# Routing of a mixture-of-experts decoder rebuilt: logits per batch in the norm, expert biases in the tile loop, slot tables in a stage of their own

## The reference, cut to what matters

```
logits = h @ W_router (+ b_router)        # 256 x 8
L0_ffn: one shared expert, 256 -> 1024 -> 256, times the sum of the top-2 weights
L1_ffn: softmax, top 2, renormalised; expert e: (silu(h@W1a+b) * (h@W1b+b)) @ W2[e] + b2[e]
L2_ffn: softmax over all, top 2 kept;     expert e: gelu(h@W1[e]+b1[e]) @ W2[e] + b2[e]
x = x + sum over the two chosen e of weight[e] * expert_e(h)
```

## Time and profile before

| | us |
|---|---|
| median of 3 runs | 3351.38 |
| lowest, highest | 3343.55, 3355.01 |
| profiled execution | 3345.55 |
| its span, first to last instruction | 3343.8 |
| PE busy in it | 2799.0 (84%) |
| DVE busy | 1519.8 (45%) |
| ACT busy | 1294.2 (39%) |
| mean granted clock of PE | 0.900 |

### The profile page before, as it was taken

How to read it: one execution, slowest core, us unless ns; L and a number is a source line. 1 busy time by engine, 2 the same in 40 slices (tenths; PEclk the granted TensorE clock), 3 DMA queues, 4 the chain that set the end, 5 groups by cost and what they waited for, 6 DMA issues and landing times. The chain is left out here.

```text
span 3343.8 us, 57353 instructions
## 1 busy us (share of the span) xinstructions
PE 2799.0 (84%) x18661; PEld 1999.5 (60%) x18662; DVE 1519.8 (45%) x3568; ACT 1294.2 (39%) x3845; POOL 888.0 (27%) x570
## 2 busy tenths in 40 slices
PE   5653899969785989999689977899968998889799
PEld 2352566646454555555379844566637997776466
DVE  5676788840534133333532266665652001653211
ACT  1321677731442113333222221677733332772211
POOL 2351555510001022222113324454521221430000
PEclk8876999979898999999769977999976999898899
DMA  2000100000241010000236620100033555003000
GB/s 100 1 1 1 35 14 14 7 16 12 52 111 31 4 37 15 10 14 7 79 121 236 222 66 7 45 19 18 14 129 104 177 184 165 8 13 107 27 25 22
DMA packets 107205, 189.63 MB, mean 57 GB/s; under 512 B 56020, under 2 KB 81316, under 8 KB 95316
## 3 DMA queue, kind: packets, MB, share of 16 engines
q1 hardware_dynamic: 92834, 162.10, 15.3%
q0 software_dynamic: 6816, 18.62, 1.9%
q10 hardware_dynamic: 7442, 7.47, 0.8%
HBM read 169.46 MB, written 18.71 MB: 56 GB/s over the span
## 5 line engine op out<-in xcount | busy, mean ns | idle before, releaser
L1319 POOL TENSOR_TENSOR L_xattn_p<-L_xattn_p,L_xattn_ri 112x1500 f32<-112x1500 f32 (+1 forms) x192 | 435.8, 2270 | 640.3 <-DVE L_xattn_ri L1577 640.3
L1475 ACT ACTIVATE L_xattn_pT<-ps 125x448 f32<-125x448 f32 (+1 forms) x576 | 254.4, 476 | 371.0 <-PE ps L1393 370.7
L1487 ACT ACTIVATE L_xattn_p<-L_xattn_sa,L_xattn_ng 112x375 f32<-112x375 f32 x512 | 305.0, 598 | 70.4 <-DVE L_xattn_ng L1606 51.7
L1393 PEld LDWEIGHTS ps<-ident,L_xattn_p 112*125 112x125 f32 x1920 | 253.1, 190 | 115.4 <-ACT L_xattn_pT L1475 35.4
L1393 PE MATMUL ps<-ident,L_xattn_p 112*125 112x112 f32 x1920 | 294.7, 284 | 21.2 <-ACT L_xattn_pT L1475 11.3
L979 PEld LDWEIGHTS ps<-L_ffn_xsT,L_ffn_w 128*128 128x128 f32 x2240 | 265.5, 195 | 7.5 <-ACT L_ffn_xsT L1009 2.3
L979 PE MATMUL ps<-L_ffn_xsT,L_ffn_w 128*128 128x128 f32 x2240 | 266.5, 278 | 2.8 <-ACT L_ffn_xsT L1009 2.8
L267 POOL TENSOR_TENSOR ln_rstd<-ln_tmp,half 112x8 f32<-112x8 f32 x26 | 44.3, 1720 | 785.4 <-DVE ln_tmp L220 596.3
L1041 DVE COPY L_ffn_y<-ps 128x256 f32<-128x256 f32 x70 | 29.7, 424 | 374.9 <-PE ps L988 374.9
L988 PE MATMUL ps<-L_ffn_weights,L_ffn_hT 128*128 x840 | 192.9, 380 | 2.1 <-DVE L_ffn_hT L1052 2.1
L278 PE MATMUL ps<-ident,ln_xn 112*128 112x112 f32 x416 | 97.9, 395 | 108.8 <-DVE ln_xn L247 94.3
(11 more groups left out here) (403 smaller groups left out, 5266.5 us busy)
## 6 DMA issues: line engine op xcount, KB each, us to landing
L_ffn_w<-in_L_ffn_experts SPq DMA_DIRECT2D x74, 1024.0 KB, 5.1
L_attn_toeplitz<-L_attn_h SPq DMA_DIRECT2D x4, 3136.0 KB, 22.7
L_xattn_src<-in_ctx SPq DMA_DIRECT2D x32, 281.2 KB, 2.9
L_ffn_weights<-in_L_ffn_experts SPq DMA_DIRECT2D x8, 1028.0 KB, 15.0
L_xattn_src<-in_ctx SPq DMA_DIRECT2D x16, 375.0 KB, 3.0
L_xattn_keys<-in_ctx SPq DMA_DIRECT2D x16, 281.2 KB, 6.7
L_xattn_rows<-in_ctx_rows SPq DMA_DIRECT2D x16, 281.2 KB
L_ffn_weights<-in_L_ffn_experts SPq DMA_DIRECT2D x8, 516.0 KB, 8.5
```

The source lines that it names most:

```text
L1319: g.tensor_tensor(P[:, m % 4, :, :], P[:, m % 4, :, :], ri[:, m % 4, :].unsqueeze(2).broadcast_to([T, W, S2]), ALU.mult).then_inc(s["prob_ ...
L1393: last = pe.transpose(turned(t)[:, j * T:(j + 1) * T], P[:, m % 4, j, kc * KW:(kc + 1) * KW], k.ident[0:T, 0:T])
L1475: act.activation(PT[:, m % 4, kc, :, :].rearrange("p h t -> p (h t)"), turned(t), ACT.Copy).then_inc(s["pt_ev_a"].sem, 1)
L1487: last = act.activation(P[:, n % 4, j, :], at, ACT.Exp, bias=ng[:, n % 4, j:j + 1], scale=-1.0 if mask else 1.0, accum_out=rs[:, n % 4, j: ...
```

## The change

- The norm: with `keep` and no learned scale DVE writes each batch once, straight into `keep`, and PE turns it from there. PE's part is written out instead of looped in these norms and in L0_ffn's. With `per_batch`, PE makes the logits of a batch two batches later, with the batch's turned tokens stationary (112 columns) and the 8 router columns moving, into PSUM bank 6; before the first it waits for the pack.
- `router` keeps only the comparison and the gates; DVE takes the logits from bank 6, adding the bias, which the pack now holds on all partitions.
- `add_second_biases` serves L0_ffn alone. In the routed layers b2 of all experts lies in the pack on all 128 partitions (2048 columns instead of 256), and DVE adds it to each tile's result in `expert_tiles`.
- `list_rows` is the table block alone. In it SP issues the first two first-weight loads and POOL, once the rows stand, the first two row fetches.
- The slots' weights are computed at the start of `expert_tiles`, and ACT makes one unit matrix a tile there, 35 in all.

```diff
@@ layer_norm @@
+        direct = keep is not None and not two_pows
+        xn = None if direct else sb("ln_xn", [T, 4, D])
...
+                        if direct:
+                            v.tensor_scalar(keep[:, b * D:(b + 1) * D], xin, mv[:, 2 * b:2 * b + 1],
+                                            scale[:, b:b + 1], ALU.subtract, ALU.mult).then_inc(ndone.sem, 1)
+                            continue
                         v.wait_ge(*ntr.at(b - 3))
...
+                if direct or per_batch is not None:
+                    lag = 2
+                    for b in range(B + lag):
+                        if b < B:
+                            turn(b, b % 4)
+                        if per_batch is not None and b >= lag:
+                            if b == lag:
+                                pe.wait_ge(*k["pack_in"].at(32))
+                            pe.wait_ge(*nev.at(b - lag + 1))
+                            per_batch(pe, b - lag)
...
+def logits_of(k, E, w):
+
+    def logits(pe, b):
+        for c in range(2):
+            last = pe.matmul(k.ps[0:T, 6, b * E:(b + 1) * E], k.XT[:, c, b * T:(b + 1) * T], w[:, c, :], start=(c == 0),
+                             stop=(c == 1))
+        return last
...
@@ router, on vector @@
-                with v.Fori(0, G // 2) as i:
-                    for u in range(2):
-                        v.wait_ge(*tr.at(2 * i + u + 1))
-                        v.tensor_copy(lg[:, bass.ds((2 * i + u) * GB, GB), :],
-                                      chunks(k.ps[0:T, 2 + u, 0:GB * E], GB)).then_inc(lgd.sem, 1)
-                v.wait_ge(*lgd.at(G))
+                of = chunks(k.ps[0:T, 6, 0:B * E], B)
+                if bias is None:
+                    v.tensor_copy(lg[:, :, :], of)
+                else:
+                    v.tensor_tensor(lg[:, :, :], of, bias.unsqueeze(1).broadcast_to([T, B, E]), ALU.add)
...
+def list_rows(k, route, consts, ahead):
...
+            @block.sync
+            def _(sp):
+                ahead["weights"](sp)
+
+            @block.gpsimd
+            def _(g):
+                g.wait_ge(*s["rg_rows"].at(1))
+                ahead["rows"](g)
+
+            @block.tensor
+            def _(pe):
+                for c in range(4):
+                    pe.wait_ge(*s["rg_hot"].at(c + 1))
+                    for n in range(c * part, (c + 1) * part):
+                        last = pe.matmul(k.ps[0:KT, 6, 0:2 * (most - 1)], place[:, n, :],
+                                         owned[:, n, :, :].rearrange("p w q -> p (w q)"), start=(n == 0),
+                                         stop=(n == picks - 1))
+                last.then_inc(s["rg_listed"].sem, 1)
...
@@ place_tokens @@
-                for n in range(PICKS):
-                    ch.link(v.tensor_tensor(hit[:, :, :], slot[:, :, :],
-                                            pick[:, n:n + 1, :].broadcast_to([T, E, B]), ALU.is_equal))
-                    ch.link(v.tensor_tensor(hit[:, :, :], hit[:, :, :], g3, ALU.mult))
-                    ch.link(v.tensor_reduce(route.weight[:, n, :], by_token(hit), AX.X, ALU.add))
                 ch.link(v.tensor_tensor(two[:, :], pick[:, 1, :], pick[:, 0, :], ALU.is_gt))
-                v.tensor_tensor(route.weight[:, 1, :], route.weight[:, 1, :], two[:, :], ALU.mult)
...
+    def first_weights(sp):
+        for t in range(2):
+            load_first(sp)(t, t)
+
+    def first_rows(g):
+        g.wait_ge(*s["rg_put"].at(16))
+        for t in range(2):
+            fetch(g)(t)
...
@@ expert_tiles @@
-                for n in range(PICKS):
-                    for b in range(B):
-                        act.activation(shares[:, n, b, :], k.ident[0:T, 0:T], ACT.Copy,
-                                       scale=route.weight[:, n, b:b + 1])
+                    act.activation(shares[:, bass.ds(t, 1), :].rearrange("p n t -> p (n t)"), k.ident[0:T, 0:T],
+                                   ACT.Copy, scale=route.weight[:, bass.ds(t, 1)])
+
                 copy_tokens(0, 0)
+                act.wait_ge(*s["rg_weighed"].at(1))
                 in_turn(act, step)
...
                 def copy_y(t, u):
+                    e = expert(mybir.EngineType.DVE, t)
                     v.wait_ge(*s["rg_down"].at(t + 1))
...
-                    v.tensor_copy(y[:, u, :], k.ps[:, 6 + u, 0:D]).then_inc(s["rg_y"].sem, 1)
+                    v.tensor_tensor(y[:, u, :], k.ps[:, 6 + u, 0:D], b2[:, bass.ds(e * D, D)], ALU.add).then_inc(
+                        s["rg_y"].sem, 1)
...
@@ host_ffn, L1_ffn @@
-        small = dict(router=by_rows(w["Wr"]), router_b=w["br"][:, None], b2=w["b2"])
+        small = dict(router=by_rows(w["Wr"]), router_b=on_rows(w["br"]), b2=on_rows(w["b2"]))
```

More of the change, by code:

```diff
@@ L443, in feed_forward, with router @@
                   down_added=n * GB, exp_in0=16 * ((experts + 1) // 2), exp_in1=16 * (experts // 2))
-def router(k, E, w, bias, gates, mode):
+def logits_of(k, E, w):
+    def logits(pe, b):
+        for c in range(2):
+            last = pe.matmul(k.ps[0:T, 6, b * E:(b + 1) * E], k.XT[:, c, b * T:(b + 1) * T], w[:, c, :], start=(c == 0),
+                             stop=(c == 1))
+        return last
+    return logits
+def router(k, E, bias, gates, mode):
     nc = k.nc
@@ L556, in add_second_biases @@
         gT = k.tile(ctx, "gates_turned", [n_g, B, T], F32)
-        if route is not None:
-            picks, part = PICKS * B, PICKS * B // 4
-            most = route.tiles + 2
-            sb = lambda n, sh: k.tile(ctx, n, sh, F32)
-            past, rest, place = sb("past", [T, picks, most]), sb("rest", [T, picks]), sb("place", [T, picks, KT])
-            owned = sb("owned", [T, picks, 2, most - 1])
-            chosen = route.pick[:, :, :].rearrange("p n b -> p (n b)")
-            spare = k.tile(ctx, "spare", [KT, most - 1], F32)
-            marks, ranks, ids, spares = consts
-            along = lambda ap, n: ap.unsqueeze(2).broadcast_to([T, ap.shape[1], n])
         with k.nc.Block(no_gpsimd_drain=True) as block:
@@ L569, in _ @@
             def _(pe):
-                def biases(i):
+                pe.wait_ge(*s["gs_copied"].at(1))
+                for q in range(B // 4):
+                    for j in range(4):
+                        last = pe.transpose(k.ps[0:n_g, q, j * T:(j + 1) * T], gs[:, 4 * q + j, :],
+                                            k.ident[0:T, 0:T])
+                    last.then_inc(s["gt_tr"].sem, 1)
+                for i in range(B // 2):
                     b = 2 * i
@@ L672, in sub_ffn @@
     gates = k.tile(ctx, name + "_gates", [T, spec["experts"] * B], F32)
-    layer_norm(k, pack=(tile, dram, lay["_total"]))
+    E = lay["router"][2] // 2 if "router" in lay else None
+    layer_norm(k, pack=(tile, dram, lay["_total"]), per_batch=E and logits_of(k, E, chunks(p("router"), 2)))
     if spec["mode"] == "fixed":
@@ L761, in __init__ @@
         self.rows = k.tile(ctx, "rows", [KT, 2, self.tiles + 1], mybir.dt.int32)
-        self.weight = k.tile(ctx, "weight", [T, PICKS, B], F32)
+        self.weight = k.tile(ctx, "weight", [T, self.tiles], F32)
+        self.slot = k.tile(ctx, "slot_f", [T, E, B], F32)
         self.expert = k.tile(ctx, "expert", [1, self.tiles + 2], mybir.dt.int32)
@@ L874, in place_tokens, with tile_loads, expert, load_first @@
         k.advance(rg_const=2, rg_chosen=1, rg_counted=1)
-def expert_tiles(k, route, name, weights, dram, layout, hidden, gated, act_fn, shares):
+def tile_loads(k, route, xs, w1, dram, layout):
+    nc, s = k.nc, k.signals
+    first_cols = layout["w1"][2]
+    w_in, x_in = [s["rg_w0"], s["rg_w1"]], [s["rg_in0"], s["rg_in1"]]
+    def expert(eng, t):
+        return nc.values_load(route.expert[0:1, bass.ds(t, 1)], engines=[eng], min_val=0,
+                              max_val=layout["_experts"] - 1,
+                              skip_runtime_bounds_check_because="place_tokens clamps it to the experts")
+    def load_first(sp):
+        def load(t, u):
+            e = expert(mybir.EngineType.SP, t)
+            sp.wait_ge(*s["rg_up"].at(2 * t - 2))
+            sp.dma_start(w1[:, u, :, :].rearrange("p c n -> p (c n)"),
+                         dram[bass.ds(e, 1), :, 0:first_cols].rearrange("e p n -> (e p) n")).then_inc(
+                             w_in[u].sem, 16)
+        return load
+    def fetch(g):
+        def one(t):
+            g.wait_ge(*s["rg_turned"].at(t - 1))
+            g.indirect_dma_start(xs[:, t % 2, :], None, k.rows_x[:, :],
+                                 bass.IndirectOffsetOnAxis(ap=route.rows[:, 0, t:t + 1], axis=0)).then_inc(
+                                     x_in[t % 2].sem, 16)
+        return one
+    def first_weights(sp):
[5 more added lines that the diff above has]
+            fetch(g)(t)
+    return dict(expert=expert, load_first=load_first, fetch=fetch, weights=first_weights, rows=first_rows)
+def expert_tiles(k, route, name, weights, layout, hidden, gated, act_fn, shares, xs, w1, ahead, b2, gates):
```

(5 more changed lines are left out.)

219 lines of the change are left out of this document (85 added, 134 removed).

## The result

The changed kernel takes 3301.83 us (median of 4 runs, 3298.93 to 3302.60), the kernel before 3347.47 on the same chip (4 runs, 3341.96 to 3355.01): a ratio of 0.9861, 95% interval 0.9837 to 0.9884, faster by 45.6 us. Its profiled execution took 3302.05 against 3345.55 before, 43.5 less.

A forecast was written before the change was run, and what follows sets the result against it. PE was taken to bound the routed tile loop (172.87 of 175 us busy), leaving the openings to gain. L0 +3.6, L1 -19.2, L2 -17.6 and L2_attn -7.1 make -40.3; put on the median, 3311 us, range 3290 to 3331.

The forecast's parts named there:

- Part 1: L0, L1, L2 norms: logits at the half clock, 1.12 us a batch; comparison +3.6, -0.3, +1.1 us.
- Part 2: L2_attn's norm, without logits: DVE writes once, 6.3 us against 10.8, -4.5; the following products -2.6.
- The clock's -2.6: Products behind L2_attn's norm: seven passes of 0.75 us instead of 0.37 at the half clock go, -2.6 us.
- Part 3: Placing in L1 and L2: slot-weight instructions leave the chain for the tile block, hidden there; -2.2 us each.
- Part 4: Table block of L1 and L2: without bias products PE's 64 passes stand in one run; -10.8 us each.
- Part 5: Rows to first product: weights and row fetches issued ahead; -5.9 us in L1, -5.7 in L2.
- Part 6: Tile loop: ACT's unit matrix and DVE's b2 addition per tile hidden in waits; zero.
- A: Rival: the logits lift the clock in the norms, 18 to 27 us less, 3284 to 3293; chance 0.15.
- B's strong form: Rival: pack lands with the last weights in L1 and L2, 9 and 18 us lost, 3338; B's chance together 0.19.
- C: Rival: tile loop's additions fall on PE's chain, 0.81 us a tile, 57 us, 3368; chance 0.05.
- D: Rival: no difference, PE's work drains at each semaphore in 48 batches, 29 us lost, 3340; chance 0.03.

The follow-up runs named there:

- x3_written_twice: Changed kernel, but DVE writes each batch twice again in L1, L2 and L2_attn; 3311.18 us.
- x2_grouped: Changed kernel with the logits taken out of the norm, four batches at once in the router block as before the change; 3297.03 us.
- x6_adds_back: Changed kernel with bias products, evictions and additions back between the tables in L1 and L2, and the tile loop copying instead of adding; 3323.78 us.
- x7_thrice: Changed kernel with two more unused b2 additions on DVE and two more unused unit matrices on ACT per tile; 3309.11 us.
- x1_logits_last: Changed kernel with all logits of a norm behind all its transposes instead of two batches behind each; 3291.82 us.
- c3_swapped: Changed kernel with logits operands swapped: 8 router columns stationary, 112 tokens moving, still per batch in the norm, turned back in the router block; 3310.75 us.

## Why the prediction was right

The forecast was 3311 us, range 3290 to 3331; measured 3301.83, a gain of 45.6 on the medians against the 40.3 recorded, and of 43.5 between the profiled executions. Of the 9.2 us between forecast and measurement 5.8 come from putting the sum on the median of three runs of the kernel before, 5.8 us above its profiled execution; 2.4 are the net of the stages below, whose errors partly cancel; the last 1.0 is in untouched stages. By its steps:

- **Part 1, logits in the norm: the mechanism right, two terms too big.** The clock stayed at 0.50 in all three layers, a pass cost 0.187 (0.19 recorded), and PE took over from DVE as the late one, which x3_written_twice confirms. But a batch took 1.04 us, not 1.12, because I added the transposes' 0.36 to the passes' 0.76 as they stood. In the mixture the first logits pass starts 0.41 us after the first transpose, and the four passes then take 0.63 (starts 0.07, 0.19, 0.19 and 0.19 apart): the first pass behind the transposes costs 0.07, while the transposes cost a little more than I had. That is 1.1 us of L1's and L2's 2.1 and 2.4 us, and L0's 0.9. The rest is the pack: first logits 3.2 us after the first transposes in L1 and 3.35 in L2 where I had 4.3 and 4.7. (Between the two landings named, 1372 KB come out at 1631.8, not 1632.0.)
- **Part 2, L2_attn:** the norm -4.6 for -4.5. The clock's -2.6 did not come in this execution, which gave 1.0. The transposes did raise the clock, 3.5 us after they began (1933.1), but it was back at 0.50 when L2902 began (1936.56), 1.3 us after the last of them, and four of its passes took 0.75 us, where none was forecast and seven did before. The size itself was right. Ten of the experiments (all but x3_written_twice) have this part unchanged: in seven of them (x2_grouped's row stands last below) the clock stayed up and the stretch took 13.74 us, 2.7 less than before; in three, as here, it fell, and the stretch took 15.4. What decides between the two is not shown.

```profile
1929.69 5.54 PE L284 MATMUL ps<-ident,L_attn_u 112*128 112x112 f32 x32 [5.52 <-DVE L_attn_u L247]
1936.56 13.96 PE L2902 MATMUL ps<-XT,L_attn_pack 128*128 x32 [1.33 <-PEq L193]
```

```profile
1932.00:1935.00 3.00, 2.86 (x22) 2.44 (x20) 2.48 (x8) 2.65 (x9) 0.00 (x0) 0.81 0.30 126
1935.00:1938.00 3.00, 1.67 (x4) 0.86 (x4) 1.67 (x4) 1.06 (x5) 0.00 (x0) 0.76 0.03 5
1938.00:1941.00 3.00, 3.00 (x7) 1.41 (x6) 2.83 (x6) 0.63 (x1) 0.00 (x0) 0.67 0.00 0
1941.00:1944.00 3.00, 3.00 (x10) 1.51 (x9) 0.18 (x1) 1.27 (x2) 0.00 (x0) 1.00 0.00 0
```

```profile
1937.89 12.29 PE L2937 MATMUL ps<-XT,L_attn_pack 128*128 x32 [1.29 <-PEq L193]
```

- **Part 3, placing:** -2.2 each, to the digit; in the tile block the weights are done by 1696.96, before the tokens land at 1697.8.
- **Part 4, tables alone:** -10.9 for -10.8, and x6_adds_back alone gives it back.
- **Part 5, fetches ahead:** the size nearly right (-5.4 for -5.9 and -5.7), its inner step wrong. I had the fetch landing in 3 us and POOL's issues holding the block; the block opened at once, and it was the landing, 3.7 us, that PE waited for. The two errors nearly cancelled, which is luck. That ACT's 32 matrices no longer lie before its first copy stood in the prediction as a remark without a number; the rows show that the gain needs it.
- **Part 6, the tile loop:** 0 recorded, +0.3 and +0.6 measured, within what the loop wanders. Covers as recorded; x7_thrice shows how much is left of them.
- **The rivals.** A (a higher clock) did not occur with these operands. The rule behind it, that a TensorE kept busy reaches the full clock (the Trainium skill, page "TensorE: Matmul & The Clock Gate", section "Why this matters for your kernels"), did not hold here for the norms or for the 13.93 us run of L624, busy throughout at 0.50. B's strong form fell: PE began its logits 5.9 us after the pack's second issue, not with the last weights. C and D fell. The chances of the cases that are faster, 0.58, 0.15 and 0.19, are 0.92 together, not 0.91.

The forecast held because each term was read from a row of the same kind; what it lacked was the question whether the moved logits should have been moved. x2_grouped shows 11.7 us left lying there, by its three stretches.

## What to carry to other kernels

Before work is moved into the shadow of another engine, price it at the clock that the mixture will get, from rows of this kernel with the same operands, and compare it with what the freed engine alone would give: here the single write was worth 6 to 7 us a layer in L1 and L2, and the interleaved logits gave most of it back. Between blocks, look for work that two engines hand back and forth: taking the bias products out of the table block was the largest gain, at no cost that shows where they went. When several engines wait at the opening of a stage, look at each one's last end, since an earlier arrival on one path is worth only what the next one leaves. And small tables of whole numbers don't need fp32; bf16 in exact parts took 8.46 us out of each table stage.

## What the runs showed of the hardware that I had not expected

- The granted clock fell with PE busy all the time: in x1_logits_last from 1.00 to 0.50, 3.5 us after the last transposes, while passes with 8 moving columns ran back to back. The passes' starts went from 0.098 to 0.187 us apart.
- Swapping the operands of the same product brought the clock to 1.00 (c3_swapped). A batch then took 1.41 us at the half clock and 0.83 at the full one, against 1.04 unswapped at the half clock; each change between transposes and products cost 0.32 us at the half clock, 0.19 unswapped.
- With the same instructions the clock can differ from one execution to the next: behind L2_attn's transposes PE paused for 1.2 to 1.4 us in every kernel, and the clock was back at 0.50 after it in four of the eleven traces with the single write, not in the other seven. It was worth 1.7 us.
- Both at the half clock and with 128 stationary columns, bf16 products with 108 moving columns started 0.09 us apart (8 in 0.90, with the last one's own latency), fp32 ones with 72 moving columns, two passes each, 0.43 (64 passes in 13.93).
- An indirect DMA issued in one block didn't hold that block open: DVE began the next one 0.7 us before POOL's second issue.
